# Layer 2's gelu as the tanh of a polynomial, in a four-layer attention kernel

## The chip, the cores and the metric

The kernel runs on one core of one Trainium2 chip. The metric is the device time of one execution in microseconds; several executions give a median. In the profile the engines are PE (TensorE matmul), PEld (its weight loads), DVE (VectorE), ACT (ScalarE), POOL (GpSimd) and SP (SyncE, which here only issues DMAs).

## The reference

Four layers in a row work on x (4 batches, 512 rows, 256 columns, float32). Layer 0 is a state-space block followed by cross attention. Layer 1 is cross attention with a two-layer network behind it. Layer 2 is cross attention with 16 heads and a gelu. Layer 3 is cross attention followed by a scan over the 512 rows, in which each step needs the one before. The part that the change touches:

```python
def _L2_xattn_ref(q, kv, ...):
    qn = layer_norm(q, q_norm_g, q_norm_b)
    kvn = layer_norm(kv, kv_norm_g, kv_norm_b)
    ...                                   # 16 heads of 16 columns
    attn = jax.nn.softmax(scores, axis=-1)
    ctx = jnp.einsum('bhqk,bhkd->bhqd', attn, V)
    ...
    return q + jax.nn.gelu(ctx @ Wo + bo, approximate=False)

# layer 3, its scan
def step(s, u_t):
    s = jax.nn.silu(s @ A.T) + u_t
    return (s, s)
```

The gelu is the exact one: h/2 times (1 + erf(h/sqrt 2)).

## The kernel before, in words

The first 345 us compute keys and values for all layers and layer 0's state-space block. What follows, up to about 1408 us, is the attention loop, and the change lies in it. The last 100 us are the scan of the last 128 rows, by itself.

**Tiling.** The 512 rows are cut into four parts of 128 rows. Within a part the stages run over layer 0 to 3, and within a layer over the four batches b = 0 to 3. A stage handles its heads four at a time. Such a group of four heads is called a quad here: two quads a stage in layers 0, 1 and 3, four in layer 2, 160 quads in all. Below, "L2 b1 quad 2" is the third quad of layer 2, batch 1.

**A quad.** PE computes the scores of four heads into four PSUM banks (L1694, all heads of a quad in one go). DVE takes the maxima: banks 0 and 1 each by itself (L1249), banks 2 and 3 together (L1252). ACT computes the four exponentials (L790). PE turns each 128x512 block of weights (L1320 is the helper), DVE copies heads 0 and 1 to SBUF (L1269), ACT copies heads 2 and 3 (L797). PE multiplies with the values (L1723). The scores of the next quad go to the same four banks, so they wait until all four exponentials and both DVE copies are done (L1688, L1689).

**Order of the engines' programs.** Each engine's instructions are in one fixed order. In the loop over quads there are two places in every quad where the *chains* go on: an even half (`chains.at(2 * Q)`, before the quad's maxima and exponentials) and an odd half (`chains.at(2 * Q + 1)`, on DVE after the maxima and before the first copy, on ACT between the second and the third exponential). A chain is what comes after a stage's attention: division by the sums, output projection, adding, normalising, projection to the next layer's queries. `after_steps` gives each step of a chain its half, counted from the chain's start, and all engines use that table. The last chain of a stage starts at the even half of the next stage's first quad, so that a layer 2 chain's step 4 lies in the next stage's quad 2. Two chains in a row use different PSUM banks and row buffers (b mod 2).

**Layer 2's chain.** At step 3 DVE adds the bias to the projection's output and writes `orows` (L1218). At step 4 ACT computes gelu (L757). At step 5 DVE adds it to the row (L1167 by L1221) and takes the mean and variance (L876, L878, L880); POOL computes the inverse root (L431). At step 6 DVE normalises (L885), at 7 ACT copies the turned rows (L713), at 8 it copies the queries (L726).

**The scan.** In parts 1 to 3 the scan of the part before runs along, one step per quarter of a quad: a small matmul on PE (L1677), tanh on ACT (L782), an operation on DVE (L1232). It stands in the three engines' orders between the other operations. Part 0 has no scan.

**Tables.** ACT's functions come in table sets. Where an activation needs another set than the last, the compiler puts an ACT_TABLE_LOAD before it. Exponential and tanh are used in turn with no load between them; gelu has another set, so a load stands before each gelu (on L757) and one before the exponential that follows (on L790).

## Time and profile before

| | |
|---|---|
| median of 3 runs | 1515.5 us (1513.93 to 1517.46) |
| profiled execution: its own time | 1517.49 us |
| profiled execution: span | 1515.9 us |
| PE busy | 1346.9 us, 89% |
| DVE busy | 1039.8 us, 69% |
| ACT busy | 1065.2 us, 70% |
| POOL busy | 82.9 us, 5% |
| mean granted clock of TensorE | 0.961 |

The busy shares are averages over stages with different limits. The span is that of the profiled execution, from its first instruction to its last; the execution's own time is 1.6 us longer, and 2.0 us above the median. PE's busy time contains its short waits between matmuls, as the profile models their ends.

### The profile page before, as it was taken

The numbers are of one execution on the slowest core, as the hardware profiler recorded it, in microseconds if no ns is written. First come the engines' busy times: TensorE is split into PE (matmuls) and PEld (weight loads), VectorE is DVE, ScalarE is ACT, GpSimd is POOL, SyncE is SP. The second block draws the span as 40 slices with busy tenths as digits, with TensorE's granted clock in tenths as the row PEclk, the third lists the DMA queues.
The fourth block names the chain that finished last, engine by engine and source line by source line (L and its number), as shares of the span: only waits on it lengthen the run. The fifth ranks groups of instructions, "written<-read, shape, count | busy, mean of one in ns | idle before, by whom it ended". The sixth has DMA issues, their size and how long they took to land.

```text
span 1515.9 us, 35932 instructions
## 1 busy us (share of the span) xinstructions
PE 1346.9 (89%) x13436; PEld 1002.6 (66%) x13436; DVE 1039.8 (69%) x2323; ACT 1065.2 (70%) x3212; POOL 82.9 (5%) x145
## 2 busy tenths in 40 slices
PE   7999899988998889999888999988899999788855
PEld 6788666665675556777666677766676777566644
DVE  4676757756787778687777777877776787777400
ACT  4556677757788887777787677777866777787422
POOL 2000111110000000000000000000000000000000
PEclk9999999999999999999999999999999999999855
DMA  8222310012221122121101211201121121110100
GB/s 296 85 87 98 103 56 2 1 46 95 58 85 42 44 75 68 42 71 57 57 30 57 83 31 58 85 29 54 47 70 43 43 85 57 29 50 9 43 0 14
DMA packets 69883, 90.42 MB, mean 60 GB/s; under 512 B 5520, under 2 KB 58896, under 8 KB 69328
## 3 DMA queue, kind: packets, MB, share of 16 engines
q1 hardware_dynamic: 69600, 87.87, 18.2%
q8 instruction: 108, 1.77, 0.5%
q14 instruction: 63, 0.52, 0.1%
q0 software_dynamic: 112, 0.26, 0.1%
HBM read 71.33 MB, written 16.78 MB: 58 GB/s over the span
## 4 chain that ended last, share of the span: by engine, by line
PE 60%; DVE 14%; ACT 14%; issue 10%; POOL 0%; DMA 0%; ACTq 0%; DVEq 0%; SPq 0%; POOLq 0%
PE ps L1320 14%; PE ps L1694 11%; PE ps L1327 8%; PE ps L1334 7%; PE ps L1723 6%; ACT arena L790 5%; DVE arena L1269 5%; PE ps L1768 3%; PE ps L1397 2%; PE ps L1521 2%; PE ps L1538 2%; PE ps L1677 2%; DVE arena L949 2%; ACT R L850 1%; DVE nmax L1252 1%
## 5 line engine op out<-in xcount | busy, mean ns | idle before, releaser
L1320 PE MATMUL ps<-W,arena 128*128 128x128 f32 x2896 | 434.6, 284 | 22.3 <-ACT arena L790 19.8
L1320 PEld LDWEIGHTS ps<-W,arena 128*128 128x128 f32 x2896 | 324.9, 145 | 171.5 <-issue 129.5
L790 ACT ACTIVATE arena<-ps,nmax 128x512 f32<-128x512 f32 x640 | 435.1, 686 | 0.2
L797 ACT COPY arena<-ps 128x512 f32<-128x512 f32 x320 | 187.3, 585 | 213.0 <-PE ps L1320 208.9
L1249 DVE TENSOR_REDUCE nmax<-ps 128x1 f32<-128x512 f32 x320 | 206.1, 686 | 119.5 <-PE ps L1694 83.3
L1269 DVE COPY arena<-ps 128x512 f32<-128x512 f32 x320 | 213.8, 686 | 23.7 <-PE ps L1320 13.5
L1694 PE MATMUL ps<-W,arena 32*128 32x512 f32 x1280 | 185.2, 646 | 35.3 <-DVE arena L1269 34.2
L1723 PE MATMUL ps<-arena 128*32 128x128 f32 x5120 | 173.4, 276 | 31.6 <-ACT arena L797 31.4
L1252 DVE TENSOR_REDUCE nmax<-ps 128x2 f32<-128x1024 f32 x160 | 193.7, 1210 | 0.0
L1723 PEld LDWEIGHTS ps<-arena 128*32 128x32 f32 x5120 | 130.4, 110 | 69.5 <-ACT arena L797 59.1
L790 ACT ACTIVATION_READ_ACCUMULATOR arena<-ps,nmax 128x1 f32 x640 | 131.1, 205 | 0.0
L1232 DVE SCALAR_TENSOR_TENSOR R<-th,ps 64x4 f32<-64x4 f32 x384 | 56.6, 147 | 87.6 <-ACT th L782 85.2
L1677 PEld LDWEIGHTS ps<-R,at 128*128 128x128 f32 x576 | 88.1, 193 | 35.5 <-DVE R L1232 33.2
L431 POOL TENSOR_TENSOR st<-st,W 128x1 f32<-128x1 f32 x80 | 44.0, 550 | 1155.2 <-DVE st L880 1146.1
L1677 PE MATMUL ps<-R,at 128*128 128x4 f32 x576 | 92.3, 231 | 11.9 <-DVE R L1232 9.1
L1327 PE MATMUL ps<-arena,W 128*128 128x128 f32 x704 | 97.2, 284 | 5.1 <-ACT arena L713 3.0
L1334 PE MATMUL ps<-W,arena 128*128 128x256 f32 x352 | 95.3, 393 | 3.8 <-ACT arena L751 3.2
L1327 PEld LDWEIGHTS ps<-arena,W 128*128 128x128 f32 x704 | 86.2, 194 | 10.4 <-ACT arena L713 8.3
L1694 PEld LDWEIGHTS ps<-W,arena 32*128 32x128 f32 x1280 | 53.7, 185 | 52.5 <-issue 40.3
L1768 PE MATMUL ps<-R,W 64*64 64x4 f32 x256 | 46.9, 252 | 32.6 <-ACT R L850 32.6
L782 ACT ACTIVATE th<-ps 64x4 f32<-64x4 f32 x384 | 64.1, 167 | 11.8 <-PE ps L1673 7.5
L1334 PEld LDWEIGHTS ps<-W,arena 128*128 128x128 f32 x352 | 60.5, 190 | 16.0 <-issue 5.9
(240 smaller groups left out, 1648.0 us busy)
## 6 DMA issues: line engine op xcount, KB each, us to landing
W<-keys SPq DMA_DIRECT2D x48, 512.0 KB, 3.7
arena<-values SPq DMA_DIRECT2D x48, 512.0 KB, 5.1
keys<-W SPq DMA_DIRECT2D x16, 448.0 KB, 3.0
...
```

The lines of the kernel that those rows point to most:

```text
L790: nc.scalar.activation(Pr[:, a, :], ps[:, a, :], ACT.Exp, bias=nmax[:, u % 32:u % 32 + 1], accum_out=den[:, u % 32:u % 32 + 1]).then_inc(s ...
L797: nc.scalar.copy(PT[:, (4 * Q + a) % 8, :, :].rearrange("p k n -> p (k n)"), psT).then_inc(sem("u_ev_act"), 1)
L1249: nc.vector.tensor_reduce(nmax[:, (u + g) % 32:(u + g) % 32 + 1], ps[:, g, :], AX, ALU.max, negate=True).then_inc(sem("u_mx"), 1)
L1252: nc.vector.tensor_reduce(nmax[:, u % 32:u % 32 + 2], ps[:, 2:4, :], AX, ALU.max, negate=True).then_inc(sem("u_mx"), 1)
L1269: nc.vector.tensor_copy(PT[:, (4 * Q + a) % 8, :, :].rearrange("p k n -> p (k n)"), ps[:, a, :]).then_inc(sem("u_ev_dve"), 1)
L1320: ins = nc.tensor.transpose(dst[:, k * P:(k + 1) * P], src[:, k * P:(k + 1) * P], ident)
L1327: ins = mm(dst[:, g * P:(g + 1) * P], w(wname, KD)[:, kk, g * P:(g + 1) * P], src[:, kk, :], start=kk == 0, stop=kk == KD - 1)
L1334: ins = mm(dst, src[:, kk, :], w(wname, parts)[:, kk, at_col:at_col + n], start=kk == 0, stop=kk == parts - 1)
L1677: mm(psR[:, NB * j:NB * (j + 1)], at2[:, :], R2[:, j, :], start=False, stop=True, skip_group_check=True).then_inc(sem("r_z"), 1)
L1694: ins = mm(ps[:, g, :], qT[b][rows, q, :], Ks[G % 4][rows, l.key_group(q), :], start=True, stop=l is not L0)
L1723: ins = mm(psT[32 * g:32 * g + 32, 0:P], Vs[G % 4][:, kt, first:first + 32], PT[:, (4 * Q + g) % 8, kt, :], start=kt == 0, stop=kt == NCH - 1)
L1768: mm(psR[0:S3, NB * j:NB * (j + 1)], W[0:S3, a3:a3 + S3], R2[0:S3, j, :], start=False, stop=True, skip_group_check=True).then_inc(sem("e_z ...
```

## The change

The polynomial is called *bend* in the code. The tanh is an ACT instruction of 128x256, like the gelu before.

- For batches 0, 1 and 2 of each part POOL computes the bend, at step 3 (14 instructions of 128x256, each waiting for the one before). ACT's tanh comes at step 8 in place of the gelu's step 4, and all later steps of the chain are four halves (two quads) later: the sum and statistics at 9, normalising at 10, the turned rows at 11, the queries at 12.
- For batch 3 DVE computes the bend, at step 3 right behind the bias (9 instructions of 128x256). The tanh stays at step 4, and the later steps stay too.
- The sum of row and gelu was one DVE instruction. It is two now: (tanh + 1) times `orows`, then 0.5 times that plus the row.
- The three buffers of each of two sides lie in W, in the space of layer 0's input weights, which nothing reads any more at that time.

```diff
+ERF_AT = 5.7
+ERF_TANH = (0.7978849414816304, ..., 1.7562063102252576e-09)      # seven
+ERF_OPS = 2 * len(ERF_TANH)
-def after_steps(li):
+def after_steps(li, b):
-                 2: dict(gelu=4, stats=5, nrm=6, tp=6), ...
+                 2: dict(gelu=8, stats=9, nrm=10, tp=10) if b < 3 else dict(gelu=4, stats=5, nrm=6, tp=6), ...
@@ POOL
+            def bend(c, b):
+                x, x2, r = bent[b % 2]
+                n = 3 * c + b
+                done = itertools.count(ERF_OPS * n + 1)
+                if n:
+                    pool.wait_ge(sem("L2_gelu"), c * NB + b + 1 - 1)
+                pool.wait_ge(sem("L2_pre"), c * NB + b + 1)
+                nc.gpsimd.tensor_scalar(x, orows[b % 2], ERF_AT, -ERF_AT, ALU.min, ALU.max).then_inc(sem("L2_bent"), 1)
+                pool.wait_ge(sem("L2_bent"), next(done))
+                nc.gpsimd.tensor_tensor(x2, x, x, ALU.mult).then_inc(sem("L2_bent"), 1)
+                pool.wait_ge(sem("L2_bent"), next(done))
+                nc.gpsimd.tensor_scalar(r, x2, ERF_TANH[-1], ERF_TANH[-2], ALU.mult, ALU.add).then_inc(sem("L2_bent"), 1)
+                for a in ERF_TANH[-3::-1]:
+                    ...                    # wait, r = r * x2, wait, r = r + a
+                ...                        # wait, r = r * x
@@ POOL, chain_of
+                if li == 2 and b < 3:
+                    yield step["add"]
+                    bend(c, b)
@@ ACT, chain_of
                     yield step["gelu"]
-                    act.wait_ge(sem("L2_pre"), n)
-                    nc.scalar.activation(nrm[i], orows[i], ACT.Gelu).then_inc(sem("L2_gelu"), 1)
+                    if b < 3:
+                        act.wait_ge(sem("L2_bent"), ERF_OPS * (3 * c + b + 1))
+                        ...
+                    else:
+                        act.wait_ge(sem("row_sum"), BENT_SUMS[c])
+                        nc.scalar.activation(bent[i][2], bent[i][2], ACT.Tanh).then_inc(sem("L2_gelu"), 1)
@@ DVE
+            def bend(c, rows, x, x2, r):
+                ...
+                nc.vector.tensor_scalar(x, rows, ERF_AT, -ERF_AT, ALU.min, ALU.max).then_inc(sem("row_sum"), 1)
+                done()
+                nc.vector.tensor_tensor(x2, x, x, ALU.mult).then_inc(sem("row_sum"), 1)
+                done()
+                nc.vector.tensor_scalar(r, x2, ERF_TANH[-1], None, ALU.mult).then_inc(sem("row_sum"), 1)
+                done()
+                for m in range(len(ERF_TANH) - 2, 0, -1):
+                    nc.vector.scalar_tensor_tensor(r, r, ERF_TANH[m], x2, ALU.add, ALU.mult).then_inc(sem("row_sum"), 1)
+                    done()
+                nc.vector.scalar_tensor_tensor(r, r, ERF_TANH[0], x, ALU.add, ALU.mult).then_inc(sem("row_sum"), 1)
@@ DVE, chain_of
+                    if b == 3:
+                        bend(c, orows[i], *bent[i])
                     yield step["stats"]
                     dve.wait_ge(sem("L2_gelu"), n)
-                    add_more(row, row, nrm[i])
+                    own["sums"] += 2
+                    nc.vector.scalar_tensor_tensor(orows[i], bent[i][2], 1.0, orows[i], ALU.add, ALU.mult).then_inc(sem("row_sum"), 1)
+                    dve.wait_ge(sem("row_sum"), own["sums"] - 1)
+                    nc.vector.scalar_tensor_tensor(row, orows[i], 0.5, row, ALU.mult, ALU.add).then_inc(sem("row_sum"), 1)
```

The instruction order shows what moves. First ACT in part 1, around batch 0's gelu, in the kernel before. ps<-arena copies (L797) are the turned weights of heads 2 and 3, L782 is the scan's tanh.

```order
L797 COPY arena<-ps 128x512
L782 ACTIVATE th<-ps 64x4
L757 ACT_TABLE_LOAD
L757 ACTIVATE arena<-arena 128x256
L797 COPY arena<-ps 128x512
L782 ACTIVATE th<-ps 64x4
L790 ACT_TABLE_LOAD
L790 ACTIVATE arena,den<-ps,nmax 128x512 x2
```

The same batch in the kernel after (L837 is the copy, L822 the scan's tanh, L830 the exponential, L794 the new tanh), two quads later in the program:

```order
L837 COPY arena<-ps 128x512
L822 ACTIVATE th<-ps 64x4
L794 ACTIVATE W<-W 128x256
L837 COPY arena<-ps 128x512
L822 ACTIVATE th<-ps 64x4
L830 ACTIVATE arena,den<-ps,nmax 128x512 x2
```

The tanh stands at the same place within a quad as the gelu did, between the two copies, and both table loads are gone. In all, ACT has 6 table loads after and 38 before.

Second, DVE at the statistics of part 1, batch 0, in the kernel before (L1249 and L1252 are the maxima, L1232 the scan, L1269 the copies of heads 0 and 1):

```order
L1252 TENSOR_REDUCE nmax<-ps 128x2
L1262 SCALAR_TENSOR_TENSOR arena<-ps,W,arena 128x128
L1232 SCALAR_TENSOR_TENSOR R<-th,ps 64x4
L1167 TENSOR_TENSOR arena<-arena 128x256
L876 BN_STATS st<-arena 128x6
L878 BN_AGGR st<-st 128x2
L880 TENSOR_SCALAR st<-st 128x1
L1269 COPY arena<-ps 128x512
```

And after (L1320 the maxima, L1300 the scan, L1286 and L1288 the two instructions of the sum, L1337 the copy):

```order
L1320 TENSOR_REDUCE nmax<-ps 128x2
L1330 SCALAR_TENSOR_TENSOR arena<-ps,W,arena 128x128
L1300 SCALAR_TENSOR_TENSOR R<-th,ps 64x4
L1286 SCALAR_TENSOR_TENSOR arena<-W,arena 128x256
L1288 SCALAR_TENSOR_TENSOR arena<-arena 128x256
L916 BN_STATS st<-arena 128x6
L918 BN_AGGR st<-st 128x2
L920 TENSOR_SCALAR st<-st 128x1
L1337 COPY arena<-ps 128x512
```

The group has one instruction more. For batch 0 it stood in L2 b1 quad 2 and stands now in L2 b2 quad 0; for batch 1 it moves from L2 b2 quad 2 to L2 b3 quad 0, for batch 2 from L2 b3 quad 2 to L3 b0 quad 0.

Third, DVE at L3 b0 quad 1, part 0, where batch 3's bias is added, in the kernel before:

```order
L1252 TENSOR_REDUCE nmax<-ps 128x2
L1218 TENSOR_TENSOR arena<-ps,W 128x256
L1269 COPY arena<-ps 128x512 x2
L1182 RECIPROCAL rden<-den 128x8
```

And after:

```order
L1320 TENSOR_REDUCE nmax<-ps 128x2
L1280 TENSOR_TENSOR arena<-ps,W 128x256
L1219 TENSOR_SCALAR W<-arena 128x256
L1221 TENSOR_TENSOR W<-W 128x256
L1223 TENSOR_SCALAR W<-W 128x256
L1226 SCALAR_TENSOR_TENSOR W<-W 128x256 x5
L1228 SCALAR_TENSOR_TENSOR W<-W 128x256
L1337 COPY arena<-ps 128x512 x2
L1244 RECIPROCAL rden<-den 128x8
```

Nine instructions stand between the maxima and the copies for which the next quad's scores wait.

## Rows read from the trace of the kernel before

**Rows 1.** The page, busy time: engine, us (share of the span) xinstructions.
```profile
PE 1346.9 (89%) x13436; PEld 1002.6 (66%) x13436; DVE 1039.8 (69%) x2323; ACT 1065.2 (70%) x3212; POOL 82.9 (5%) x145
```

**Rows 2.** Groups by line, ACT: busy us, mean ns | idle before.
```profile
L757 ACT ACT_TABLE_LOAD x16 | 20.5, 1283 | 0.3
```

**Rows 3.** Timeline of ACT in L2 b2 quad 2, part 1: start us, us.
```profile
762.02 1.28 ACT L757 ACT_TABLE_LOAD   x1
763.31 0.42 ACT L757 ACTIVATE arena<-arena 128x256 f32<-128x256 f32 x1
...
764.28 1.28 ACT L790 ACT_TABLE_LOAD   x1
765.58 0.69 ACT L790 ACTIVATE arena<-ps,nmax 128x512 f32<-128x512 f32 x1
```

**Rows 4.** Timeline of PE and ACT in L2 b3 quad 1, part 1.
```profile
782.23 1.14 PE L1694 MATMUL ps<-W,arena 32*128 32x512 f32 x8 [0.21 <-DVE arena L1269]
...
784.00 0.59 ACT L797 COPY arena<-ps 128x512 f32<-128x512 f32 x1 [1.41 <-PE ps L1320]
...
784.55 0.67 ACT L790 ACTIVATE arena<-ps,nmax 128x512 f32<-128x512 f32 x1
```

**Rows 5.** Timeline of DVE in L2 b2 quad 2, part 1.
```profile
767.18 0.41 DVE L1167 TENSOR_TENSOR arena<-arena 128x256 f32<-128x256 f32 x1
767.63 0.43 DVE L876 BATCH_NORM_STATS2 st<-arena 128x6 f32<-128x256 f32 x1
...
768.38 0.69 DVE L1269 COPY arena<-ps 128x512 f32<-128x512 f32 x1
```

**Rows 6.** Windows, one quad each: length, PE, PEld, DVE, ACT, POOL busy, PEclk, DMA.
```profile
755.67:761.75 6.08, 5.65 (x68) 4.18 (x69) 4.54 (x11) 4.59 (x15) 0.00 (x0) 1.00 0.37 135
761.75:769.88 8.13, 5.42 (x68) 3.95 (x68) 5.88 (x16) 7.53 (x19) 0.55 (x1) 1.00 0.00 0
769.88:776.37 6.49, 5.89 (x74) 4.63 (x74) 4.67 (x12) 4.33 (x15) 0.00 (x0) 1.00 0.01 3
776.37:782.23 5.86, 5.09 (x68) 3.92 (x68) 4.67 (x12) 5.05 (x17) 0.00 (x0) 1.00 0.20 48
```

**Rows 7.** Windows, quads of part 0 (no scan).
```profile
486.31:491.86 5.55, 4.47 (x59) 2.97 (x58) 4.38 (x8) 4.82 (x13) 0.00 (x0) 1.00 0.16 30
497.52:504.45 6.93, 4.80 (x58) 2.95 (x58) 5.60 (x12) 6.79 (x14) 0.55 (x1) 1.00 0.01 2
541.66:547.32 5.66, 5.28 (x60) 3.49 (x61) 4.20 (x9) 4.04 (x12) 0.00 (x0) 1.00 0.46 161
567.03:573.50 6.47, 6.26 (x68) 4.15 (x67) 5.47 (x12) 4.99 (x15) 0.55 (x1) 1.00 0.31 94
```

**Rows 8.** Windows, L3 b0 quad 1 and L3 b1 quad 0 of part 1.
```profile
808.88:814.97 6.09, 5.66 (x69) 4.21 (x69) 4.53 (x12) 4.45 (x15) 0.00 (x0) 1.00 0.38 126
814.97:823.21 8.24, 5.52 (x68) 4.05 (x69) 5.62 (x15) 7.64 (x20) 0.55 (x1) 1.00 0.42 128
```

**Rows 9.** Groups by line and form, DVE and POOL.
```profile
L1167 DVE TENSOR_TENSOR arena<-arena 128x256 f32<-128x256 f32 x16 | 6.6, 410 | 0.0
L1238 DVE SCALAR_TENSOR_TENSOR SS<-R,UT 64x512 f32<-64x512 f32 x3 | 2.0, 683 | 0.1
L963 DVE COPY cm<-W 64x256 f32<-64x256 f32 x1 | 0.3, 277 | 0.0
L444 POOL TENSOR_TENSOR SS<-SS 128x256 f32<-128x256 f32 x2 | 1.5, 726 | 0.2
```

**Rows 10.** Windows, quads behind a gelu with a lower clock, parts 1 and 2.
```profile
788.18:796.64 8.46, 6.62 (x68) 5.33 (x68) 6.07 (x17) 7.03 (x18) 0.55 (x1) 0.80 0.01 3
1037.37:1045.69 8.32, 6.57 (x67) 5.22 (x68) 6.06 (x17) 6.90 (x18) 0.55 (x1) 0.80 0.00 0
1045.69:1053.59 7.90, 7.51 (x75) 5.34 (x75) 4.56 (x11) 4.86 (x17) 0.00 (x0) 0.78 0.01 2
```

**Rows 11.** Timeline of POOL and DVE before the attention loop; then DVE alone.
```profile
173.00 4.20 POOL L477 TENSOR_TENSOR dAm<-UT,W 128x1024 bf16<-128x1024 bf16 x2 [14.99 <-DVE UT L1023]
173.57 1.88 DVE L949 SCALAR_TENSOR_TENSOR arena<-arena,W 128x512 f32<-128x512 f32 x1
...
27.27 2.32 DVE L949 SCALAR_TENSOR_TENSOR arena<-arena,W 128x512 f32<-128x512 f32 x3
```

More of the change, by code:

```diff
@@ L132 @@
 CUTS = [0] + [PLAN[name][0] for name in ("wk0", "wv0", "inw", "wq0")] + [NPACK]
-def after_steps(li):
+ERF_AT = 5.7
+ERF_TANH = (0.7978849414816304, 0.03633308446488688, -3.2594837808075025e-05, -5.5306259012116404e-05,
+            3.964757753935919e-06, -1.322645093331823e-07, 1.7562063102252576e-09)
+ERF_OPS = 2 * len(ERF_TANH)
+BENT_SUMS = (23, 56, 89, 122)
+def after_steps(li, b):
     step = dict(rd=0, rdT=1, on=2, wo=2, add=3)
     step.update({0: dict(tp=3), 1: dict(f_tp=3, f_xT=4, f_h=4, bias=5, f_relu=5, f_o=5, stats=6, nrm=7, tp=7),
-                 2: dict(gelu=4, stats=5, nrm=6, tp=6), 3: dict(bias=2, stats=3, nrm=4, tp=4)}[li])
+                 2: dict(gelu=8, stats=9, nrm=10, tp=10) if b < 3 else dict(gelu=4, stats=5, nrm=6, tp=6), 3: dict(bias=2, stats=3, nrm=4, tp=4)}[li])
     tp = step["tp"]
@@ L307, in build @@
         orows = [a3.take(D) for _ in range(2)]
+        spare = Carve(W[:, PLAN["inw"][0]:PLAN["outw"][0]])
+        bent = [[spare.take(D) for _ in range(3)] for _ in range(2)]
         oT = [a3.take(4 * P).rearrange("p (q n) -> p q n", q=4) for _ in range(2)]
@@ L500, in _ @@
             pool.memset(UT[:, 0, :], 0.0).then_inc(sem("zeroed"), 1)
+            def bend(c, b):
[11 more added lines that the diff above has]
+                for a in ERF_TANH[-3::-1]:
+                    pool.wait_ge(sem("L2_bent"), next(done))
+                    nc.gpsimd.tensor_tensor(r, r, x2, ALU.mult).then_inc(sem("L2_bent"), 1)
+                    pool.wait_ge(sem("L2_bent"), next(done))
+                    nc.gpsimd.tensor_scalar(r, r, a, None, ALU.add).then_inc(sem("L2_bent"), 1)
+                pool.wait_ge(sem("L2_bent"), next(done))
+                nc.gpsimd.tensor_tensor(r, r, x, ALU.mult).then_inc(sem("L2_bent"), 1)
             def chain_of(o, b):
@@ L506, in chain_of @@
                     return
-                n, step = turn_side(G), after_steps(li)
+                n, step = turn_side(G), after_steps(li, b)
+                if li == 2 and b < 3:
+                    yield step["add"]
+                    bend(c, b)
                 if li:
@@ L741, in chain_of @@
                 c, li, _ = STAGES[G]
-                l, i, n, step = LAYERS[li], b % 2, turn_side(G), after_steps(li)
+                l, i, n, step = LAYERS[li], b % 2, turn_side(G), after_steps(li, b)
                 if l.quads != 2 * (wq + 1):
@@ L755, in chain_of @@
                     yield step["gelu"]
-                    act.wait_ge(sem("L2_pre"), n)
-                    nc.scalar.activation(nrm[i], orows[i], ACT.Gelu).then_inc(sem("L2_gelu"), 1)
+                    if b < 3:
[3 more added lines that the diff above has]
+                        act.wait_ge(sem("row_sum"), BENT_SUMS[c])
+                        nc.scalar.activation(bent[i][2], bent[i][2], ACT.Tanh).then_inc(sem("L2_gelu"), 1)
                 if li < 3:
@@ L1168, in add, with done @@
                 dve.wait_ge(sem(name), n)
+            def bend(c, rows, x, x2, r):
+                def done():
+                    own["sums"] += 1
+                    dve.wait_ge(sem("row_sum"), own["sums"])
+                if c:
+                    dve.wait_ge(sem("L2_gelu"), NB * c)
+                dve.wait_ge(sem("L2_pre"), NB * (c + 1))
+                nc.vector.tensor_scalar(x, rows, ERF_AT, -ERF_AT, ALU.min, ALU.max).then_inc(sem("row_sum"), 1)
[8 more added lines that the diff above has]
+                nc.vector.scalar_tensor_tensor(r, r, ERF_TANH[0], x, ALU.add, ALU.mult).then_inc(sem("row_sum"), 1)
+                own["sums"] += 1
+                assert own["sums"] == BENT_SUMS[c], (c, own["sums"])
             def add_more(dst, src, other):
@@ L1176, in chain_of @@
                 c, li, _ = STAGES[G]
-                l, i, n, step = LAYERS[li], b % 2, turn_side(G), after_steps(li)
+                l, i, n, step = LAYERS[li], b % 2, turn_side(G), after_steps(li, b)
                 X, row, res = psX[i], xrow[b], RES[:, c * NB + b, :]
@@ L1580, in chain_of @@
                 c, li, _ = STAGES[G]
-                l, i, n, step = LAYERS[li], b % 2, turn_side(G), after_steps(li)
+                l, i, n, step = LAYERS[li], b % 2, turn_side(G), after_steps(li, b)
                 X = psX[i]
```

2 lines of the change are left out of this document (added).

## The prediction, as it was written before the result was known

> **What bounds the kernel now.** I read the page's busy times first. PE is busy 89% of the span, DVE 69%, ACT 70% [rows 1]. POOL's 5% says only that it has room. The shares do not say who is late in a quad, so I next read the timeline of single quads, and then windows cut at each quad's first score matmul.
>
> A quad is a closed loop. The next scores need this quad's banks, hence all exponentials and both DVE copies. In a plain quad of the scan parts the scores start at 782.23 and the first exponential at 784.55, 2.32 us later. ACT sat idle 1.41 us in that stretch, waiting for PE's turned block [rows 4]. A plain quad lasts 5.86 us, and one whose even half has the gelu and whose odd half has the statistics 8.13 [rows 6].
>
> What the gelu costs: in its quad the scores start at 761.75 [rows 6] and the first exponential at 765.58 [rows 3], 3.83 us later in place of 2.32. Two loads of 1.28 and the activation's 0.42 are 2.98 us of ACT, of which ACT's idle time swallows about half; 1.51 us reach the loop.
>
> What DVE work in an odd half costs: from 765.58 to the next scores at 769.88 are 4.30 us. The group of sum and statistics lies from 767.18 to 768.38, directly ahead of the first copy, which PE's scores wait for [rows 5, 6]. So 1.20 us of it stand in a stretch of 3.10 us without it. A quad with D us of DVE work in the odd half then lasts 2.32 + 3.10 + D = 5.42 + D. In part 0 a quad with the same 1.20 us and no gelu lasts 6.47 [rows 7], so there it is 5.27 + D. An instruction of 0.3 to 0.4 us still fits: the quad with only the bias add is 6.08, 0.22 above the plain one [rows 6].
>
> **The change part by part.**
>
> *Loads and gelu.* 16 loads of 1.283 us [rows 2] and as many as long ahead of the exponential [rows 3] are 41 us of ACT time. At 1.51 us a gelu, at most 16 x 1.51 = 24 us of it lie on the path. The new tanh (0.42 us like the gelu, same form) stands at an even half, behind the same idle 1.41 us; I cost it at nothing. In L3 b1 quad 0 it shares that place with batch 2's queries (two 128x128 activations, about 0.6 us): 1.0 us in all, still under 1.41.
>
> *Statistics, batches 0 to 2.* The group moves to the next stage's quad 0 and gains an instruction. A row sum costs 0.45 us from start to start [rows 5]. A scalar_tensor_tensor of 256 columns lies between 0.41 and 0.68 us (a tensor_tensor at 256 columns and the same form at 512) [rows 9]. The nearer in size is the first; I take 0.42, plus 0.04 of issue. Two of them are 0.92 for 0.45, so D = 1.20 + 0.47 = 1.67. The copy of turned rows on ACT (the 6.49 quad, 0.63 over plain) moves from quad 3 to quad 1, where it lies beside the bias add on DVE. Per batch in the scan parts [rows 6]: quad 0 from 5.86 to 7.09, quad 1 from 6.08 to 6.49, quad 2 from 8.13 to 5.86, quad 3 from 6.49 to 5.86. That is +1.23 + 0.41 - 2.27 - 0.63 = -1.26 us, nine times: -11.3 us.
>
> In part 0 the gelu quad is 6.93 and the plain one 5.55 [rows 7]. Quad 0 becomes 5.27 + 1.67 = 6.94 (+1.39), quad 2 loses 1.38. Nothing is won: there the gelu's wait had let DVE finish its maxima, and hid the statistics. Three times 0.
>
> *Batch 3.* The bend on DVE: two tensor_scalar, bounded by 0.28 (a copy of 256 columns within SBUF) [rows 9] and 0.41, taken as 0.33; one tensor_tensor 0.41; six scalar_tensor_tensor 0.42; each plus 0.04: 0.74 + 0.45 + 2.76 = 3.95 us. With the bias add D = 4.40 in L3 b0 quad 1. In the scan parts that quad goes from 6.09 [rows 8] to 9.82, +3.73. Batch 2's turned rows (0.41 in the list above) go under it on ACT, -0.41. The gelu quad behind it, 8.24 [rows 8], loses 1.51 and gains 0.47. Sum +2.28, three times: +6.8. In part 0: 5.66 [rows 7] to 9.67 is +4.0, turned rows -0.6, the gelu quad's 6.93 becomes 6.94: +3.4. Bounds for the nine instructions: 3.5 us (all at 0.35) and 4.9 us (0.50 each), so -1.8 to +3.8 us over four parts.
>
> *POOL's bend.* Seven tensor_tensor of 128x256 at 0.73 us [rows 9]; the seven tensor_scalar lie between nothing and 0.73, taken as 0.40; with 0.1 us between instructions 9.3 us, at most 11.6. From step 3 to step 8 are five halves, over 14 us. POOL's roots come before or after it. Hidden; its cover fails at 1 us per instruction.
>
> *Clock.* TensorE's granted clock fell to half behind some gelus, when PE had waited through the loads: 0.80 and 0.78 in windows where it is otherwise 1.00. One such place cost 8.46 - 8.13 = 0.33 us, another 0.19 + 7.90 - 6.49 = 1.60 [rows 6, 10]. Four of the 16 gelus have one; at 1.0 each, 4 us go with the loads. In the four bend quads PE stands still for almost 4 us in one piece, longer than behind a gelu. I count three of four with the full 1.6: +4.8. Net +0.8; bounds -4 and +11 (all four, each over two more quads). The Trainium skill (TensorE: Matmul & The Clock Gate, "Why this matters for your kernels") advises against gaps between matmul bursts because the clock drops to half; the rows on the gelu quads agree.
>
> *Contention.* While POOL worked on 128x1024, a DVE operation with two SBUF inputs took 1.88 us; three of the same form elsewhere took 2.32 together, 0.77 each [rows 11]. So a POOL instruction can hold one of DVE's. During POOL's bend DVE runs mostly maxima and copies out of PSUM. Of the SBUF-to-SBUF kind there is one copy per bend (L1187, at an even half, ahead of maxima that wait for PE anyway). 12 waits of at most 0.73 behind idle time: 0 to 8.8 us, taken as +0.4. The Trainium skill (SBUF — State Buffer, "Who interferes with whom") says that only DVE instructions with two SBUF inputs or in a two-port mode exclude POOL's. By that rule this term stays near my value; without it, see the second rival.
>
> *Sum.* -11.3 + 6.8 + 3.4 + 0.8 + 0.4 = +0.1 us on the profiled execution's own 1517.5 us, which is 2.0 above the median. On the median: 1515.5 + 0.1 = 1515.6 us.
>
> **The rivals.**
>
> 1. *The work moved onto DVE is hidden, faster.* DVE has 30% idle; if the statistics in quad 0 and the second instruction cost only half of what I charge, then 9 x 0.61 + 3 x 0.7 + 4 x 0.2 = 8.4 us less: 1507 us. For it: the bias add costs 0.22 of its 0.41. Against: 1.20 us cost 0.92 in the part-0 quad without a gelu (6.47 against 5.55) [rows 7]. 22%.
> 2. *Contention, slower.* If every DVE instruction with an SBUF operand waits for POOL's running one, some 16 per bend wait about 0.3 us: nearly 5 us a bend, twelve bends, up to 58 us; if only one in six waits, 10 us: 1525. It decides as soon as DVE's copies out of PSUM (0.69) [rows 5] are longer on the mean. Against: they read PSUM and not SBUF. 10%.
> 3. *Clock, slower.* The stall of a bend leaves PE at half clock through two quads each time, so 4 x 3 us rather than 4.8: +7, 1523 us. For it: after 1037.37 two quads in a row were slow. 14%.
> 4. *POOL late, slower.* Over 1 us an instruction and ACT waits for the bend twelve times: 14 x 0.1 x 12 = 17 us for each tenth over it. 4%.
>
> **How the numbers follow.** 50% is left for the forecast, whose own range is 1511.5 to 1520 (bounds of the bend and of the clock term). What a measurement here can tell from no change is 0.2%, 3 us: 1512.5 to 1518.5. Of the forecast's 50%, 38 lie within, 5 below, 7 above; the rivals leave 4 more within. So faster 25%, same 42%, slower 33%. The range that should hold the time 8 times in 10 is 1508 to 1524.
>
> **What would show it.** Right: six table loads on ACT; the first exponential 2.3 us after the scores in the former gelu quads; L2 b2 quad 0 near 7.1 us in parts 1 to 3 and L3 b0 quad 1 near 9.8; DVE's nine instructions near 3.95 us, PEclk below 1 right behind them; POOL's bend near 9 us. Wrong: copies of 0.69 us getting longer during POOL's bend (rival 2), quad 0 near 6.4 (rival 1), ACT's tanh behind a wait for POOL (rival 4).

## The result, and the profile after

| | before | after |
|---|---|---|
| median, first measurement | 1515.3 us (1513.9 to 1517.5, 4 executions) | 1535.3 us (1525.4 to 1540.5, 4) |
| median, measured again | 1517.1 us (1512.2 to 1521.6, 25) | 1526.4 us (1518.0 to 1533.6, 10) |
| profiled execution: own time, span | 1517.5, 1515.9 us | 1530.3, 1528.7 us |
| mean granted clock of the 14 executions after (59 of before) | 0.959 to 0.967 | 0.943 to 0.964 |

The change makes the kernel slower: ratio 1.0124 (95% interval 1.0099 to 1.0149) in the first measurement, 1.0072 (1.0049 to 1.0095) in the second, so 9 to 20 us where +0.1 was forecast. The time of after also scatters over 22 us, that of before over 10. One execution of the kernel before took 1733 us at a mean clock of 0.737 and is left out everywhere.

The page of after, busy time; its answer is [rows 1]:

```profile
PE 1357.1 (89%) x13436; PEld 1010.9 (66%) x13436; DVE 1061.8 (69%) x2375; ACT 1023.3 (67%) x3180; POOL 203.6 (13%) x313
```

ACT lost 42 us of work and POOL gained 121, as the change says. PE has the same 13436 matmuls and is busy 10 us longer; in this profile 29 us more of the span ran at half clock, which fits that.

Windows of after, part 1: L2 b2 quads 0 to 3 (compare [rows 6]), then L3 b0 quad 1 with the bend on DVE and L3 b1 quad 0 behind it (compare [rows 8]); last the same two quads of part 2. Columns: length, busy time (and instructions) of PE, PEld, DVE, ACT, POOL, granted clock, DMA share, GB/s.

```profile
754.40:761.53 7.13, 5.35 (x67) 3.95 (x68) 6.17 (x17) 4.91 (x17) 0.57 (x1) 1.00 0.34 104
761.53:768.34 6.81, 6.70 (x79) 5.28 (x79) 4.96 (x13) 4.45 (x15) 1.56 (x4) 1.00 0.15 51
768.34:774.20 5.86, 5.08 (x69) 3.92 (x68) 5.24 (x12) 5.04 (x17) 5.30 (x7) 1.00 0.00 0
774.20:780.18 5.98, 4.86 (x64) 3.54 (x65) 4.36 (x11) 4.49 (x15) 3.15 (x4) 1.00 0.01 3
812.80:823.00 10.20, 6.76 (x78) 5.31 (x79) 8.33 (x21) 5.89 (x19) 0.00 (x0) 1.00 0.13 44
823.00:831.06 8.06, 7.61 (x69) 6.59 (x69) 6.04 (x16) 3.93 (x14) 0.55 (x1) 0.60 0.34 97
1090.51:1102.33 11.82, 8.38 (x79) 6.22 (x79) 8.37 (x22) 5.89 (x19) 0.00 (x0) 0.80 0.07 25
1102.33:1111.73 9.40, 8.86 (x69) 7.02 (x69) 6.01 (x16) 3.98 (x14) 0.55 (x1) 0.52 0.29 84
```

Quad 0 got the statistics (7.13), quad 2 is a plain one now (5.86 for 8.13). In quad 1 PE is busy 6.70 of 6.81 us with 79 matmuls, where it had 68 and 5.65: PE bounds this quad now. The bend quad lasts 10.20, and behind it the clock is 0.60 and 0.52.

The gelu's place, timeline of ACT in L2 b2 quad 0 (batch 0's tanh), whose scores start at 754.40; it answers to [rows 3]. Columns as in [rows 4]: start, length, engine, line, and in brackets the idle time before and what ended it.

```profile
754.54 0.41 ACT L794 ACTIVATE W<-W 128x256 f32<-128x256 f32 x1
756.16 0.58 ACT L837 COPY arena<-ps 128x512 f32<-128x512 f32 x1 [1.21 <-PE ps L1388]
...
756.71 0.68 ACT L830 ACTIVATE arena<-ps,nmax 128x512 f32<-128x512 f32 x1
```

The first exponential starts 2.31 us after the scores (3.83 with the gelu), and ACT is idle 1.21 us behind the tanh. No load is left here. Timeline of DVE in the same quad, the statistics (compare [rows 5]):

```profile
758.38 0.41 DVE L1286 SCALAR_TENSOR_TENSOR arena<-W,arena 128x256 f32<-128x256 f32 x1
758.82 0.42 DVE L1288 SCALAR_TENSOR_TENSOR arena<-arena 128x256 f32<-128x256 f32 x1
...
760.03 0.69 DVE L1337 COPY arena<-ps 128x512 f32<-128x512 f32 x1
```

From 758.38 to the copy are 1.65 us, the forecast's D of 1.67.

PE in L2 b2 quad 1, the two projections that now share it, and the next scores:

```profile
763.32 1.03 PE L1402 MATMUL ps<-W,arena 128*128 128x256 f32 x4
...
766.79 1.06 PE L1395 MATMUL ps<-arena,W 128*128 128x128 f32 x8
...
768.34 0.71 PE L1762 MATMUL ps<-W,arena 32*128 32x512 f32 x4
```

L1402 is batch 1's output projection, which always lay in quad 1. L1395 is batch 0's projection to layer 3's queries, which stood in quad 3 before. ACT and DVE are not what the last row waits for: it has no idle time ahead of it.

Timeline of DVE in L3 b0 quad 1, part 1; the first exponential of the quad starts at 815.12:

```profile
815.33 1.21 DVE L1320 TENSOR_REDUCE nmax<-ps 128x2 f32<-128x1024 f32 x1
817.23 0.15 DVE L1300 SCALAR_TENSOR_TENSOR R<-th,ps 64x4 f32<-64x4 f32 x1 [0.70 <-ACT th L822]
817.31 0.41 DVE L1280 TENSOR_TENSOR arena<-ps,W 128x256 f32<-128x256 f32 x1
817.82 0.29 DVE L1219 TENSOR_SCALAR W<-arena 128x256 f32<-128x256 f32 x1
818.15 0.43 DVE L1221 TENSOR_TENSOR W<-W 128x256 f32<-128x256 f32 x1
818.61 0.29 DVE L1223 TENSOR_SCALAR W<-W 128x256 f32<-128x256 f32 x1
818.94 2.26 DVE L1226 SCALAR_TENSOR_TENSOR W<-W 128x256 f32<-128x256 f32 x5
821.23 0.43 DVE L1228 SCALAR_TENSOR_TENSOR W<-W 128x256 f32<-128x256 f32 x1
821.58 1.28 DVE L1337 COPY arena<-ps 128x512 f32<-128x512 f32 x2
```

The nine instructions take 3.76 us to the copy (3.95 was forecast). But the group starts 2.19 us after the first exponential, against 1.60 for the statistics of [rows 3, 5]: DVE was idle 0.70 us before it.

Timeline of PE behind it:

```profile
823.00 1.14 PE L1762 MATMUL ps<-W,arena 32*128 32x512 f32 x8 [3.35 <-DVE arena L1337]
...
825.43 1.93 PE L1791 MATMUL ps<-arena 128*32 128x128 f32 x32 [0.45 <-ACT arena L837]
...
828.53 2.37 PE L1388 MATMUL ps<-W,arena 128*128 128x128 f32 x10
```

PE stood still for 3.35 us, and then 32 matmuls that take 1.08 us at full clock (764.28 in the quad above and 815.73 here) take 1.93.

**Where the 12.8 us between the two profiles lie.** The first scores of the attention loop start 3.5 us later (344.9 against 341.4), where nothing was changed; the loop is 9.0 us longer; the tail is 0.3 longer. In the loop layer 2's stages of parts 1 to 3 gain 13.8 us and part 0's gains 2.8; layer 3's, which hold batch 2's statistics and batch 3's bend, lose 17.2 and 6.8; the rest is clock at other places.

### The profile page after: what moved, and what is told of

Its sections match the earlier page's. It is cut to its first block, busy times and chain, and to the rows that moved or that the text cites. A ratio compares the mean times of both kernels' runs of the same rounds, so it can differ in the third digit from the quotient of the medians.

```text
span 1528.7 us, 36134 instructions
## 1 busy us (share of the span) xinstructions
PE 1357.1 (89%) x13436; PEld 1010.9 (66%) x13436; DVE 1061.8 (69%) x2375; ACT 1023.3 (67%) x3180; POOL 203.6 (13%) x313
## 4 chain that ended last, share of the span: by engine, by line
PE 62%; DVE 18%; ACT 10%; issue 9%; POOL 0%; DMA 0%; ACTq 0%; DVEq 0%; SPq 0%; POOLq 0%
PE ps L1388 13%; PE ps L1762 12%; PE ps L1402 8%; PE ps L1395 7%; PE ps L1791 7%; DVE arena L1337 6%; PE ps L1836 3%; ACT arena L830 3%; PE ps L1465 2%; PE ps L1589 2%; PE ps L1606 2%; DVE arena L989 2%; PE ps L1745 2%; ACT R L890 1%; DVE nmax L1317 1%
## 5 line engine op out<-in xcount | busy, mean ns | idle before, releaser
L830 ACT ACTIVATE arena<-ps,nmax 128x512 f32<-128x512 f32 x640 | 434.5, 685 | 0.0
L837 ACT COPY arena<-ps 128x512 f32<-128x512 f32 x320 | 187.3, 585 | 250.2 <-PE ps L1388 246.0
L1337 DVE COPY arena<-ps 128x512 f32<-128x512 f32 x320 | 213.7, 686 | 25.4 <-PE ps L1388 14.1
L1320 DVE TENSOR_REDUCE nmax<-ps 128x2 f32<-128x1024 f32 x160 | 193.7, 1211 | 0.0
L830 ACT ACTIVATION_READ_ACCUMULATOR arena<-ps,nmax 128x1 f32 x640 | 130.7, 204 | 0.0
L1745 PE MATMUL ps<-R,at 128*128 128x4 f32 x576 | 92.4, 231 | 15.5 <-DVE R L1300 12.5
L1300 DVE SCALAR_TENSOR_TENSOR R<-th,ps 64x4 f32<-64x4 f32 x384 | 56.4, 147 | 65.9 <-ACT th L822 63.7
L1395 PE MATMUL ps<-arena,W 128*128 128x128 f32 x704 | 97.3, 284 | 5.0 <-ACT arena L749 2.7
L1402 PE MATMUL ps<-W,arena 128*128 128x256 f32 x352 | 95.9, 395 | 3.8 <-ACT arena L787 3.1
L1395 PEld LDWEIGHTS ps<-arena,W 128*128 128x128 f32 x704 | 86.0, 194 | 10.9 <-ACT arena L749 8.8
L822 ACT ACTIVATE th<-ps 64x4 f32<-64x4 f32 x384 | 64.2, 167 | 17.4 <-PE ps L1745 9.9
L1402 PEld LDWEIGHTS ps<-W,arena 128*128 128x128 f32 x352 | 61.4, 193 | 16.1 <-issue 5.9
```

What stands on the lines that cost most here:

```text
L830: nc.scalar.activation(Pr[:, a, :], ps[:, a, :], ACT.Exp, bias=nmax[:, u % 32:u % 32 + 1], accum_out=den[:, u % 32:u % 32 + 1]).then_inc(s ...
L837: nc.scalar.copy(PT[:, (4 * Q + a) % 8, :, :].rearrange("p k n -> p (k n)"), psT).then_inc(sem("u_ev_act"), 1)
L1320: nc.vector.tensor_reduce(nmax[:, u % 32:u % 32 + 2], ps[:, 2:4, :], AX, ALU.max, negate=True).then_inc(sem("u_mx"), 1)
L1337: nc.vector.tensor_copy(PT[:, (4 * Q + a) % 8, :, :].rearrange("p k n -> p (k n)"), ps[:, a, :]).then_inc(sem("u_ev_dve"), 1)
L1395: ins = mm(dst[:, g * P:(g + 1) * P], w(wname, KD)[:, kk, g * P:(g + 1) * P], src[:, kk, :], start=kk == 0, stop=kk == KD - 1)
L1402: ins = mm(dst, src[:, kk, :], w(wname, parts)[:, kk, at_col:at_col + n], start=kk == 0, stop=kk == parts - 1)
```

## The experiments

All were compared with the kernel before, run beside them on the same chip; its medians there were 1515.7 us (experiments 1, 3, 5 and 7), 1517.1 (2, 4, 6 and 8), 1516.1 (9 to 11) and 1514.3 (12). Experiments on different chips are best compared by their ratios; 0.001 of ratio is 1.5 us. Code cuts are shortened.

**1. Only the loads gone.** What is the removal worth if nothing else moves?

```diff
 (kernel before)
-nc.scalar.activation(nrm[i], orows[i], ACT.Gelu)
+nc.scalar.activation(nrm[i], orows[i], ACT.Tanh)
```

> The kernel before with one word changed: ACT computes tanh where it computed gelu, so the 32 table loads are gone and nothing moves (the output is not a gelu). Theory S (the loop of a quad decides): the first exponential comes 1.5 us earlier in 16 quads; in the three scan parts all of it stays, in part 0 the statistics lose their cover and about 0.3 to 0.9 of it comes back. -20 to -24 us, plus some 4 us for clock drops that go with the loads: 1488 to 1496 us. Rival H (ACT is not what a quad waits for, the gain goes into other idle time): under 8 us, over 1507.

Measured: 1496.6 us (1494.2 to 1496.7, 4), ratio 0.9856 (0.9829 to 0.9882): 19 us. Window of its L2 b2 quad 2, part 1:

```profile
758.49:765.16 6.67, 5.35 (x67) 3.95 (x68) 5.74 (x16) 4.92 (x17) 0.55 (x1) 1.00 0.00 0
```

8.13 became 6.67, the 1.46 us that 1.51 had been forecast for. In part 0 the same quad goes from 6.93 to 6.47. Over all 16 quads, at full clock, it is about 20 us. So the loads alone are worth 19 us, and the change spends all of it and 9 to 20 us more.

**2. Only the move.**

```diff
 (kernel before, after_steps)
-2: dict(gelu=4, stats=5, nrm=6, tp=6)
+2: dict(gelu=8, stats=9, nrm=10, tp=10) if b < 3 else dict(gelu=4, stats=5, nrm=6, tp=6)
```

> The kernel before with only the steps moved: gelu and its two table loads stay on ACT, but at step 8, with statistics, normalising and queries four halves later, for batches 0 to 2. Theory M (the moved work loses the gelu's cover): the gelu's delay of 1.5 us stays, now in quad 0, and the statistics come right behind it as before, so only the turned rows beside the bias add change: +0.2 to +0.4 us per batch, 2 to 5 us in all, and batch 3's gelu shares its place with batch 2's queries, +1 us each: 1520 to 1524. If the move costs nothing by itself, 1513 to 1518.

Measured: 1525.6 us (1523.0 to 1529.0, 5), ratio 1.006 (1.0036 to 1.0083). Its windows: L2 b2 quads 0 and 1 and L3 b1 quad 0, part 1:

```profile
750.09:758.41 8.32, 6.52 (x67) 5.18 (x67) 6.07 (x17) 6.89 (x18) 0.55 (x1) 0.80 0.41 126
758.41:766.88 8.47, 8.36 (x80) 6.19 (x79) 4.85 (x12) 4.99 (x17) 0.00 (x0) 0.79 0.02 4
820.28:829.47 9.19, 5.53 (x69) 4.06 (x69) 5.60 (x15) 8.58 (x22) 0.55 (x1) 1.00 0.37 115
```

The move by itself costs 8 us, with the same instructions. At full clock batch 0's four quads change by +2.27, +0.73, -2.27 and -0.51: +0.2; batch 1's sum is +0.4. Batch 2 costs more, +1.0: its quad 1 falls on L3 b0 quad 1 (+0.71), and its queries on batch 3's gelu and loads (9.19 for 8.24). That is about 1.6 us a part and 6 in all; the remaining 2 to 3 us go with the clock. The median is just above the 1520 to 1524 that were expected. Quad 1 of L2 b2 or b3, in which PE now has no room, took 1.6 us more at half clock in 13 places of the eight profiles of kernels with the move (0.79 here), and in none of the six profiles without it.

**3. No bend on DVE.** Batch 3's tanh takes the clipped h: its polynomial is left out.

```diff
 (kernel after, DVE bend: eight of nine instructions out)
 nc.vector.tensor_scalar(r, rows, ERF_AT, -ERF_AT, ALU.min, ALU.max)
-(in words) x2 = x*x; r = x2*a6; five of (r + a)*x2; r = (r + a0)*x
```

> The kernel after, with batch 3's polynomial left out: of the nine VectorE instructions only the first (the clip) stays, its output goes to the tanh. Theory S: four bend quads lose 3.6 us each, 14 us. Theory C (clock): if the stall of a bend also costs by the lower clock, in this and the following quads, the loss is larger than 14 us and the half-clock time outside the tail falls from 61 us to 20 to 35 us; then 1535 - 14 - 5 to 12 = 1509 to 1516 on the median, and the runs differ by under 5 us. Without theory C 1521 and a spread as before of 15 us.

Measured: 1509.3 us (1507.4 to 1519.1, 7), ratio 0.9968 (0.9941 to 0.9995). Its L3 b0 quad 1, part 1:

```profile
809.71:816.50 6.79, 6.69 (x78) 5.28 (x79) 5.19 (x14) 4.35 (x15) 0.00 (x0) 1.00 0.23 76
```

The eight instructions cost 10.20 - 6.79 = 3.41 us in each scan part and 2.66 in part 0 (9.17, at full clock, to 6.51): 12.9 in all. By the ratios 16 us went (0.9968 against 1.0072 for after measured again, give or take 5), by the medians 17 to 26. What is over 12.9 lies within that noise, and the executions still differed by 11.7 us where under 5 were expected, so this run does not show the clock's share. Without the eight instructions PE bounds this quad too (6.69 of 6.79): 0.70 us over the 6.09 of [rows 8] are PE's, from the moved projection.

**4. Half the bend on DVE** (five instructions; the polynomial of batch 3 is cut short).

```diff
 (kernel after)
-for m in range(len(ERF_TANH) - 2, 0, -1):
+for m in (1,):
```

> The kernel after with a shorter polynomial for batch 3: four of the five middle steps on VectorE are left out, five instructions stay in place of nine (the result of batch 3 is another polynomial). The bend is 2.1 us in place of 4.0. Theory S alone: 4 x 1.85 = 7.4 us less than the kernel after. Theory C: the gap on TensorE is then about 2 us, shorter than behind a gelu with its loads; the clock stays up, and the loss is 7.4 us plus nearly all of the 12 to 15 us that the extra matmuls gave: 1511 to 1516.

Measured: 1514.4 us (1511.1 to 1529.1, 10), ratio 1.0009 (0.9978 to 1.004). The two quads of part 1:

```profile
805.29:813.66 8.37, 6.76 (x79) 5.31 (x79) 6.63 (x18) 5.79 (x19) 0.00 (x0) 1.00 0.10 37
813.66:820.89 7.23, 5.46 (x69) 4.06 (x69) 5.98 (x16) 4.46 (x15) 0.55 (x1) 1.00 0.38 114
```

Four instructions fewer are 1.83 us, 0.46 each: DVE's time reaches the loop in full. The median falls by 11.9 us and not by 4 x 1.83 = 7.3. But the ten executions scatter over 18 us, and by the ratios it is 10 us, give or take 6: that the excess over 7.3 is the clock's is not shown here. In the profile the quad right behind the bend kept its full clock in all four parts; in part 3 the bend quad itself lost 1.6 us, and L3 b1 quad 1 in parts 2 and 3 and L2 b3 quad 1 in part 3 as much each.

**5. The stall filled.** The strongest test of the clock: the same bend and the same wait, but PE computes something in it that nobody reads.

```diff
 (kernel after, PE, L3 b0 quad 1 of each part, once the exponentials are done)
+pe.wait_ge(sem("u_exp"), 4 * Q + 4)
+for _ in range(4):
+    mm(ps[:, 3, :], ident, W[:, 0:512], start=True, stop=True)
```

> The kernel after, with four extra matmuls of 128x512 on TensorE in each of the four bend quads, into a bank that is overwritten, placed where TensorE otherwise stands still while VectorE computes the polynomial. They fill about 3.4 of some 4 us. Theory C: the clock does not fall behind the bends, the quads behind them take 7.15 us in place of 8 to 9.4 and the spread over runs shrinks; 5 to 15 us less than the kernel after: 1518 to 1526. Rival (no effect of the clock; the time is VectorE's stall alone): no change within 2 us, or up to 0.5 us per bend more where the matmuls end late.

Measured: 1520.3 us (1517.0 to 1523.1, 10), ratio 1.0024 (1.0012 to 1.0035). Its two quads in part 1, and PE's timeline of the filler:

```profile
813.68:823.90 10.22, 10.13 (x87) 6.80 (x87) 8.35 (x22) 4.92 (x15) 0.00 (x0) 1.00 0.11 37
823.90:831.12 7.22, 5.45 (x69) 4.05 (x69) 6.03 (x16) 5.44 (x19) 0.55 (x1) 1.00 0.36 110
```

```profile
820.25 3.60 PE L1826 MATMUL ps<-W 128*128 128x512 f32 x8
```

The bend quad is as long as ever (10.22), the quad behind is 7.22 or 7.23 in parts 1 to 3 (6.65 in part 0), at clock 1.00. (PE's row shows 8 matmuls, two records for each of the four.) In part 0 the filler ends after DVE's copies: the bend quad lasts 9.89 there, 0.7 more than the 9.17 of after at full clock. Even so the median is 6 us below that of after's second measurement, 7 by the ratios (3 to 11), and the scatter of ten executions shrank from 16 to 6 us. So idle PE time at the bend, not the bend's length, costs those 6 or 7 us.

**6. No bend on POOL** (batches 0 to 2 get the clipped h; POOL's 14 instructions become one).

> The kernel after with GpSimd's polynomial left out for batches 0 to 2: one instruction, the clip, stays of the 14. Theory N (GpSimd holds up VectorE): the copies of 0.23 us that took up to 0.79 beside GpSimd's work are short again and the kernel gains over 3 us, 1527 to 1532, and quad 1 of L2 b2 falls below 6.81. Rival (the copy stands in VectorE's idle time, GpSimd costs nothing): quads equal within 0.1 us each, time within the spread of the kernel after.

Measured: 1525.7 us (1521.9 to 1537.1, 9), ratio 1.006 (1.0035 to 1.0085), against 1.0072 for after in the same rounds. The intervals overlap: POOL's bend costs nothing that can be measured. At full clock every quad of layer 2 is the same within 0.05 us.

**7. Batch 3 as before** (gelu and its loads, one addition on DVE).

```diff
 (kernel after, b == 3)
-act.wait_ge(sem("row_sum"), BENT_SUMS[c]); tanh(bent)
+act.wait_ge(sem("L2_pre"), n); nc.scalar.activation(nrm[i], orows[i], ACT.Gelu)
```

> The kernel after with batch 3 as in the kernel before: ACT's gelu with its two loads, no polynomial on VectorE, one instruction for the sum. Batches 0 to 2 stay with GpSimd's polynomial and the later steps. Theory S from the quads of the trace after: per batch 0 to 2 in the scan parts about -0.8 us against the kernel before, in part 0 about 0, batch 2's turned rows cost what they did: -7 us, and 3 us of clock drops that went with 12 of the 16 gelus. 1503 to 1510 us. If the later steps or GpSimd's work have a price of their own that the quads hide, over 1513.

Measured: 1518.2 us (1515.1 to 1522.7, 10), ratio 1.0012 (0.9995 to 1.0029). Better than after by 8 to 17 us, but not the 1503 to 1510 that I expected. Batch 2's queries now stand beside batch 3's loads, and that quad lasts 9.2 to 9.6 us where it was 8.24: 3.8 us over the four parts at full clock. All quads together come to -3 us against before at full clock, where +2 was measured; in this profile four of the moved quads 1 ran at half clock, 1.6 us each.

**8 and 9. After and before again.**

> The kernel after, unchanged, on the chip and in the rounds of the next three, for a comparison by runs of one chip. Theory C (the clock falls behind the bends): median 1530 to 1538, a spread of over 8 us, half-clock windows at the bend quads in this trace too. If the 15 us between the kernel after and the version with extra matmuls came from the chip, 1518 to 1524.

Measured: 1526.4 us, in the table above: between the two ranges, so neither theory's median came. The spread of 15.5 us and the slow quads at the bends are those of theory C. Quad 0 +1.27, quad 1 +0.73 or +0.88 and the bend quad +4.12 came out as in the first profile; what changed was where the clock fell, and the first scores started at 341.1 us, not 344.9.

> The kernel before, unchanged, profiled again. It says how much of a difference between two profiles is the clock's own: the first scores of the attention loop came at 341.4 us in the first profile of before and at 344.9 us in that of after, and nothing of the change lies ahead of them. If that is chance, a second profile of before gives a start elsewhere between 341 and 345 us and half-clock stretches of other places, with every quad of undisturbed clock the same within 0.05 us. If the start is at 341.4 again and the stretches lie at the same places, the later start of after would be an effect of the change.

Measured: 1516.4 us (1515.1 to 1518.0, 8), ratio 1.0001 (0.9989 to 1.0012); first scores at 342.9 (341.4 in the first profile of before). The later start of after is chance: in the profiles it goes with the time that PE spent at half clock ahead of the loop, from about 3 us of it (start at 341.1) to 14 us (344.8 to 345.4).

**10. The step that the experiments point to.** Loads are dear, moving is dear, DVE's time is dear, POOL's is free. So the bend has to be short enough for POOL to finish between step 3 and step 4, and nothing may move. Three instructions are: tanh(h(0.80025 + 0.0347 h²)), which makes the gelu differ from the exact one by at most 0.0003 (worked out, for all h).

```diff
 (kernel before, all four batches)
+ POOL, step 3: x2 = h*h; r = x2*CUBE + LINE; r = r*h      -> L2_bent
+               hx = 0.5*h; row = row + hx
+               wait for the tanh; x2 = r*hx
- ACT, step 4:  nrm = Gelu(orows)
+ ACT, step 4:  wait L2_bent; r = Tanh(r)
- DVE, step 5:  row = row + nrm
+ DVE, step 5:  row = row + x2                              (one instruction, as before)
```

> The kernel before (no step moved, nothing more on VectorE) with the gelu of all four batches as tanh(h(a + c h^2)), a cubic for the seven coefficients: POOL computes it in three instructions at step 3 and the tanh stays at step 4, where the gelu was. POOL also takes the half of h, adds it to the row while ScalarE works, and multiplies the tanh with it, so that VectorE keeps its one addition. Theory A (the whole loss of the change is what it moved and what it put on VectorE; POOL and the tanh cost nothing): the time of the kernel in which only the table loads went away, 1496.6 us, so 1494 to 1501 us. Theory B (POOL's work is itself dear in so short a place, since ScalarE has to wait for 2.0 us of POOL and VectorE for one more instruction of 0.73 us): each of 16 chains some 0.5 to 1 us later, 1505 to 1513 us, with ScalarE's tanh shown behind a wait for POOL.

Measured: **1493.0 us** (1492.2 to 1494.2, 4), ratio 0.9846 (0.9831 to 0.986): faster than both kernels. Its timeline of POOL and ACT, part 1 (scores at 758.55), and the windows of L2 b2 quad 2 and L3 b1 quad 0:

```profile
757.16 0.61 POOL L511 TENSOR_TENSOR W<-arena 128x256 f32<-128x256 f32 x1 [17.87 <-DVE arena L1241]
757.86 0.41 POOL L513 TENSOR_SCALAR W<-W 128x256 f32<-128x256 f32 x1
758.35 0.73 POOL L515 TENSOR_TENSOR W<-W,arena 128x256 f32<-128x256 f32 x1
```

```profile
759.11 0.42 ACT L780 ACTIVATE W<-W 128x256 f32<-128x256 f32 x1 [0.31 <-POOL W L515]
760.32 0.59 ACT L820 COPY arena<-ps 128x512 f32<-128x512 f32 x1 [0.79 <-PE ps L1343]
```

```profile
758.55:765.22 6.67, 5.35 (x67) 3.95 (x68) 6.04 (x16) 5.03 (x17) 3.33 (x5) 1.00 0.00 0
808.53:815.29 6.76, 5.46 (x68) 4.05 (x69) 6.05 (x15) 5.08 (x18) 3.50 (x5) 1.00 0.30 94
```

ACT does wait for POOL, 0.31 us, and is then still idle for 0.79 us until PE's turned block: the wait is free. Each quad is the same as in experiment 1 within 0.05 us, but for one that had lost 1.6 us to the clock. Theory A holds, and its 1496.6 us were even a little high.

**11. The second sum instruction alone.**

```diff
 (kernel of experiment 10: POOL keeps its first three instructions)
-DVE: row = row + x2
+DVE: orows = (r + 1)*orows;  row = 0.5*orows + row
```

> As the kernel with POOL's cubic, but with the two scalar_tensor_tensor of the kernel after on VectorE in place of the one addition and of POOL's last three instructions. It prices the second sum instruction alone. If VectorE's time in an odd half reaches the loop in full (the model 5.42 + D), 16 x 0.47 = 7.5 us slower than that kernel: about 1504 us. If the cover that the gelu's wait gave to the statistics in part 0 matters, the four there are exposed as well, so nothing changes on that. If such an instruction is half hidden: 3 to 4 us slower, 1500 us.

Measured: 1501.2 us (1500.5 to 1503.1, 4), ratio 0.9903 (0.9887 to 0.992), so 8.1 us more than experiment 10. L2 b2 quad 2, part 1:

```profile
761.98:769.11 7.13, 5.34 (x67) 3.95 (x68) 6.46 (x17) 5.03 (x17) 1.07 (x2) 1.00 0.00 0
```

All 16 such quads are 0.45 to 0.47 us longer. The model 2.32 + 3.10 + D gives 7.09 with D = 1.67, 0.04 below.

**12. One operation or two on POOL.** (In experiment 10's kernel, `hx = 0.5*h` becomes `hx = 0.5*h + 0.0`.)

> As the kernel with POOL's cubic; only the halving of h on POOL is written with two operations (times 0.5, plus 0.0) in place of one. In the kernels so far POOL's tensor_scalar of 128x256 took 0.40 to 0.41 us in its two forms with two operations and 0.85 to 0.87 in its two forms with one. If the number of operations decides, this one falls from 0.87 to about 0.41 us and POOL's last product is ready 0.46 us sooner. If it is what the instruction reads or where it stands (this one reads a row buffer while ScalarE works), it stays at 0.87. The time stays 1493 us in either case, 1491 to 1496, since VectorE's addition does not wait for POOL.

Measured: 1494.6 us (1493.7 to 1494.6, 4), ratio 0.9861 (0.983 to 0.9892). The groups of POOL by line and form, first in experiment 10 and then here:

```profile
L516 POOL TENSOR_SCALAR W<-arena 128x256 f32<-128x256 f32 x16 | 13.9, 870 | 0.0
```

```profile
L516 POOL TENSOR_SCALAR W<-arena 128x256 f32<-128x256 f32 x16 | 6.7, 417 | 0.0
```

The form with two operations takes 0.417 us, the one with one 0.870, at the same place and on the same data.

## Why the prediction was wrong

The step that failed is the clock term. The forecast set the drops that go with the gelus' loads (-4) against drops behind the bends (+4.8) and got +0.8 us; the executions show about 9. A second, smaller step failed with it: PE was left out of the price of the moved steps (2.9 us). Most other sizes were right.

- **Loads and gelu** (at most 24 us on the path): right. 1.46 a gelu in the scan parts where 1.51 was forecast; the tanh at nothing, right.
- **Statistics in quad 0**: 7.09 forecast, 7.13 measured; in part 0 +1.39 forecast, +1.38 measured. The second sum instruction is 0.46, not less; experiment 11 refutes rival 1.
- **Turned rows and queries in quad 1**: this step failed. The forecast looked at ACT's copy and DVE's bias add only, and took 6.49, the longer of the two quads that merge. But the step also carries PE's eight matmuls L1395 (1.06 us) with its turning, and the quad already had PE's output projection (1.03). PE is busy 6.70 of 6.81 us. The two extras add up: 5.86 + 0.22 + 0.63 = 6.71, plus 0.1. Per part 3.24 us are gained where 4.19 were forecast (with the 0.41 that the bend's place was to save), so 2.9 us are missing over three parts.
- **Part 0, "three times 0"**: near. Quads 2 and 3 gain 2.1 us together, quads 0 and 1 lose 2.2, so +0.15 for each of batches 0 and 1, and -0.7 for batch 2, whose quad 1 is the bend's. The part's sum is +2.9 where +3.4 was forecast.
- **The bend**: the nine instructions are 3.76 (forecast 3.95), but the quad is 10.20 (forecast 9.82). What is missing is DVE's later start, 2.19 us behind the first exponential where the model had 1.60. The moved projection cannot be its cause: it starts at 817.94, after the group (817.31). Most of it stood in the kernel before, in the same quad of part 1:

```profile
810.59 1.11 PE L1334 MATMUL ps<-W,arena 128*128 128x256 f32 x4
811.20 0.67 ACT L790 ACTIVATE arena<-ps,nmax 128x512 f32<-128x512 f32 x1
813.22 0.41 DVE L1218 TENSOR_TENSOR arena<-ps,W 128x256 f32<-128x256 f32 x1
```

  There the bias add starts 2.02 us behind the first exponential. PE's own output projection of that quad (L1334) stands ahead of the value products, and the scan's tanh, for which DVE waits, comes behind them. The 1.60 was read in a quad without that projection. So the model 5.42 + D was carried to a quad for which it does not hold: 0.38 us too little, three times. In part 0, without a scan, the bend quad is 9.17 at full clock, 0.50 less than forecast.
- **The quad behind**, 7.20 forecast (8.24 - 1.04): 7.22 with the clock kept (experiments 3 to 5), 8.06 and 9.40 in the profile of after.
- **POOL's bend**: hidden, right, though it took 11.1 us and not 9.3 (766.52 to 777.65).
- **Contention** (+0.4): nothing measurable (experiment 6). The trace does show the mechanism once more. POOL and DVE in after, part 1:

```profile
768.19 0.72 POOL L529 TENSOR_TENSOR W<-W 128x256 f32<-128x256 f32 x1
```

```profile
768.20 0.79 DVE L1249 COPY arena<-rden 128x128 f32<-128x128 f32 x1
```

  The copy takes 0.23 us elsewhere (754.39); here it ends 0.08 us behind POOL's instruction. It lies ahead of maxima that wait for PE, so it costs nothing. Rival 2 is refuted: the 48 copies out of PSUM (L1337) that ran beside POOL's bend took 0.69 us, as the others did. The rule of the Trainium skill that the prediction cites (SBUF — State Buffer, "Who interferes with whom") agrees if this copy, which has one SBUF input, runs in a two-port mode; no row says whether it does.

Sum without the clock: forecast -0.7 with contention, so -1.1 of moves and bends. At full clock I count -0.45 for parts 1 to 3 (3 x (-3.24 + 4.11 - 1.02)) and +2.9 for part 0: about +2.5 us. That is still "no change".

- **Clock**: this is what decided. Forecast: -4 with the loads, +4.8 behind the bends. The traces show two levels only (1.2 and 2.4 GHz, granted 0.50 and 1.00), so 2 x (1 - mean clock) x span is the time at half clock. Over its executions it is 112 us at the median for before and 140 for after (some 87 of each in the tail). A straight line through the 14 executions of after gives 0.32 us of span for each us at half clock, and at 118 us, what the profile of before had, 1519.2 us of span; a line through 59 executions of before gives 1516.0 there. So at equal clock after is 3.2 us slower, in line with the +2.5 of the quads, and 28 us more at half clock are another 9. Together 12; the medians say 9 to 20, and the median of all 14 is 1527.9. Experiment 5 shows that most of the 9 us hang on the stalls of the bends. With the stalls filled and every moved step still moved, the ratio is 1.0024, 3.6 us over before, and the quads at full clock alone give 2.5 + 0.7; its executions have 106 us at half clock at the median, 112 have those of before. The moved quads have a share too: the 13 slow ones counted in experiment 2, at 1.6 us each, are 2.6 us a profile (the first profile of after has one of them, the second three). Other quads may be slow less often for it, so 2.6 is an upper estimate, and an exact split of the 9 us stays open. The forecast's 0.33 us for one slow place compared that quad, L2 b3 quad 2, with another batch's 8.13; its own likes last 8.25, so it is 0.20. Of the 4 us that should go with the loads, experiment 1 shows nothing (19 us, where its quads at full clock give 20) and experiment 10 some 3 (23 for the same 20).

Rival 3 named this mechanism and gave it 14% and 7 us over the forecast. It was right in kind and too small: it counted only the two quads behind each bend, at some 1.5 us each, and no slow quads at other places. The upper bound of +11 for the clock did hold what came, but I gave it almost no weight and let the range end at 1524; the spread that a kernel with more stalls has from execution to execution was in no term. The Trainium skill (TensorE: Matmul & The Clock Gate, "What's actually happening") says that the same kernel shows a different number of slow matmuls from run to run, since the monitor runs free of the kernel; the two profiles of before, with starts at 341.4 and 342.9 us, and the 22 us between executions of after agree with it.
